# Attention and experts on one core: q and k in two float32r parts, two heads in the two row halves of TensorE, a new written-out order

## The reference

```python
qkv = x @ W_qkv                      # x: 16 x 1024 x 256
q, k = _rope(q, k)                   # per head: 1024 x 16
att = einsum('bhtd,bhsd->bhts', q, k) / sqrt(16) + causal mask
y = softmax(att) @ v                 # then heads side by side
x = layernorm(x + y @ W_o)
gate = softmax(x @ Wg + bg)          # top 2 of 8, renormalised
out = sum over experts of gate * (x @ We.T + be)
x = layernorm(x + out)
```

## Time and profile before

| what | us |
|---|---|
| median of 3 runs | 3425.34 (3417.21 to 3430.62) |
| the profiled execution | 3433.1 |
| its span | 3431.4 |
| PE busy in the span | 3291.5 (96%) |
| DVE busy | 2741.6 (80%) |
| ACT busy | 1897.2 (55%) |
| POOL busy | 1234.4 (36%) |

### The profile page before, as it was taken

How to read it: one execution, slowest core, us unless ns; L and a number is a source line. 1 busy time by engine, 2 the same in 40 slices (tenths; PEclk the granted TensorE clock), 3 DMA queues, 4 the chain that set the end, 5 groups by cost and what they waited for, 6 DMA issues and landing times.

```text
span 3431.4 us, 59169 instructions
## 1 busy us (share of the span) xinstructions
PE 3291.5 (96%) x19072; PEld 1738.4 (51%) x19072; DVE 2741.6 (80%) x8349; ACT 1897.2 (55%) x4257; POOL 1234.4 (36%) x1467
## 2 busy tenths in 40 slices
PE   5899999999999999999999999999999999999987
PEld 2234555555555555555555555555555555555555
DVE  5778887878888788888878888787888878888735
ACT  2367555564655556555564655657465564655541
POOL 4254324343333444334344332444334344432110
PEclk7799999999999999999999999999999999999998
DMA  5334343232433333343242433333343242434000
GB/s 135 59 61 81 52 84 56 45 79 48 83 52 68 59 58 70 52 84 57 50 79 42 83 57 74 57 55 69 58 78 57 52 75 50 77 52 72 2 25 13
DMA packets 174790, 210.98 MB, mean 61 GB/s; under 512 B 25992, under 2 KB 124560, under 8 KB 174224
## 3 DMA queue, kind: packets, MB, share of 16 engines
q1 hardware_dynamic: 173056, 202.98, 33.9%
q10 hardware_dynamic: 1424, 4.21, 0.3%
HBM read 138.43 MB, written 67.11 MB: 60 GB/s over the span
## 4 chain that ended last, share of the span: by engine, by line
PE 81%; DVE 9%; issue 3%; POOL 2%; DMA 2%; ACT 1%; DVEq 0%; ACTq 0%; SPq 0%; POOLq 0%
PE bank L890 22%; PE attend L983 15%; PE bank L947 13%; PE scores L963 13%; PE bank L927 6%; PE bank L1007 3%; PE bank L1045 2%; DVE bank L760 2%; PE bank L936 2%; DMA x_in<-in_x 2%; PE bank L991 1%; DVE maxima L763 1%; PE bank L915 1%; PE bank L998 1%; PE bank L1015 1%
## 5 line engine op out<-in xcount | busy, mean ns | idle before, releaser
L642 ACT ACTIVATE weights<-scores 128x512 f32<-128x512 f32 (+3 forms) x3072 | 1351.6, 494 | 1077.5 <-PE scores L963 1067.2
L760 DVE CUSTOM_DVE_ANT_0 bank<-bank,far_q 128x128 f32<-128x128 f32 (+3 forms) x2048 | 960.6, 514 | 217.2 <-PE bank L947 200.4
L963 PE MATMUL scores<-q_stack,k_stack 99*128 99x512 bf16 (+3 forms) x3072 | 826.1, 330 | 8.6 <-ACT weights L642 8.3
L947 PE MATMUL bank<-k_stack,q_stack 96*128 96x512 bf16 (+3 forms) x3072 | 792.6, 334 | 31.7 <-DMA k_stack<-parts_scratch 8.9
L559 POOL TENSOR_SCALAR_AFFINE_SELECT weights<-weights 128x512 f32<-128x512 f32 x512 | 325.3, 637 | 1201.7 <-ACT weights L642 1199.8
L763 DVE TENSOR_REDUCE maxima<-bank 128x1 f32<-128x512 f32 x1024 | 641.9, 682 | 49.0 <-PE bank L947 43.6
L983 PE MATMUL attend<-weights,v_now 128*32 128x512 f32 (+3 forms) x6144 | 660.9, 502 | 3.9 <-POOL weights L559 3.8
L963 PEld LDWEIGHTS scores<-q_stack,k_stack 99*128 99x128 bf16 x3072 | 265.7, 98 | 526.2 <-ACT weights L642 275.4
L947 PEld LDWEIGHTS bank<-k_stack,q_stack 96*128 96x128 bf16 x3072 | 271.2, 98 | 480.3 <-issue 242.2
L864 DVE SCALAR_TENSOR_TENSOR z<-bank,gates,z 128x256 f32<-128x256 f32 x512 | 247.0, 482 | 204.9 <-PE bank L890 203.6
L890 PE MATMUL bank<-wexp_hi,zT_hi 128*128 128x512 f32 x1024 | 377.2, 450 | 0.0
(11 more groups left out here) (106 smaller groups left out, 3467.2 us busy)
## 6 DMA issues: line engine op xcount, KB each, us to landing
parts_scratch<-parts SPq DMA_DIRECT2D x128, 384.0 KB, 2.5
q_stack<-parts_scratch SPq DMA_DIRECT2D x384, 128.0 KB, 7.1
k_stack<-parts_scratch SPq DMA_DIRECT2D x384, 128.0 KB, 7.6
x_in<-in_x SPq DMA_DIRECT2D x64, 256.0 KB, 3.0
z<-in_x SPq DMA_DIRECT2D x32, 512.0 KB, 5.1
out<-z SPq DMA_DIRECT2D x32, 512.0 KB, 3.4
q_stack<-maxrow SPq DMA_DIRECT2D x192, 8.0 KB, 2.1
z<-in_w_exp ACTq DMA_DIRECT2D x1, 1024.0 KB, 14.5
```

The source lines that it names most:

```text
L642: act.activation(weights[:, n % 2, hh, c0:CH], st[(QUAD * n + hh) % NS][:, c0:CH], ACT.Exp, scale=DH ** -0.5).then_inc(S["weights_ready"], 1)
L760: dve.tensor_tensor_reduce(out=b[:, 0:w], in0=b[:, 0:w], in1=far_q[:, CH - w:CH], scale=1.0, scalar=-SENTINEL, op0=ALU.add, op1=ALU.max, a ...
L947: pe.matmul(b[:, 0:w], q_stack[0:ROWS, n, hh, qt * P:(qt + 1) * P], k_stack[0:ROWS, n, hh, kc * CH:kc * CH + w], start=True, stop=True).th ...
L963: pe.matmul(st[(QUAD * n + hh) % NS][:, c0:CH], k_stack[0:MROWS, s, hh, kb * P:(kb + 1) * P], q_stack[0:MROWS, s, hh, qc * CH + c0:(qc + 1 ...
```

## The change

- Each of q and k is split into two float32r parts rather than three bf16 parts: one cast on ACT, one subtraction, which writes back into `rope`; both parts are stored, as float32, from `parts` and `rope`. The products are three rather than six: 48 rows and 2 rows of maxima, 50 rather than 99.
- A head therefore fits in 64 rows. The stacks hold heads 0 and 2 of a group in rows 0 to 63 and heads 1 and 3 in rows 64 to 127. `ST` uses the half `hh % 2`; `B` takes head `hh ^ 1`, so that it begins with the upper half.
- `LOAD` stays at 12 transfers, of 16 rows x 2 heads x 1024 float32. The maxima rows are split in two operations, not four, and written by 4 transfers, not 3.
- The copy of `QK` to `rope` waits for the store of the cast two before it, rather than for that cast's last subtraction.
- `ORDER` is written anew. Nearly every step moves by some places; maxima steps now stand more often in threes and fours, `MOE` steps in longer rows, `LOAD.0` one item earlier, `QK.1.0` seven items earlier.

The diff, cut to its core:

```diff
-TERMS = ((0, 0), (0, 1), (1, 0), (1, 1), (0, 2), (2, 0))
+TERMS = ((0, 0), (0, 1), (1, 0))
+PARTS = 2
 ROWS = len(TERMS) * DH
-MROWS = ROWS + 3
+MROWS = ROWS + PARTS
+LANE = 64
+LANES = P // LANE
+PAIRS = QUAD // LANES
...
-ST.16.0 ST.16.1 BE.0.0 ST.16.2 ST.16.3 B.1.3.1 CAST.0.3.1 B.1.3.2 B.1.3.3 PV.15 YE.1.0
-ST.17.0 B.1.4.0 ST.17.1 B.1.4.1 ST.17.2 BE.0.1 MOE.0.0.0 B.1.4.2 B.1.4.3 B.1.5.0 ST.17.3 PV.16
...
+ST.16.0 CAST.0.2 ST.16.1 ST.16.2 QK.0.3 B.1.3.3 ST.16.3 PV.15 B.1.4.0 B.1.4.1 B.1.4.2 YE.1.0
+ST.17.0 VP.2 VP.3 ROPE.0.3 GB.0 ST.17.1 B.1.4.3 B.1.5.0 B.1.5.1 ST.17.2 ST.17.3 PV.16 CAST.0.3 B.1.5.2 B.1.5.3
+  LOAD.1
+ST.18.0 ST.18.1 QK.1.0 B.1.6.0 ST.18.2 B.1.6.1 ST.18.3 PV.17 B.1.6.2 B.1.6.3 ROPE.1.0 B.1.7.0
+ST.19.0 GT.0 B.1.7.1 ST.19.1 ST.19.2 ST.19.3 PV.18 BE.0.0 BE.0.1 MOE.0.0.0 MOE.0.0.1 MOE.0.0.2 MOE.0.0.3
+  MOE.0.1.0 MOE.0.1.1 MOE.0.1.2
...
-        parts = sb("parts", [P, 2, 3, CH], BF16)
-        q_stack = sb("q_stack", [P, SLOTS, QUAD, T], BF16)
-        k_stack = sb("k_stack", [P, SLOTS, QUAD, T], BF16)
+        parts = sb("parts", [P, 2, CH], F32R)
+        q_stack = sb("q_stack", [P, SLOTS, PAIRS, T], F32R)
+        k_stack = sb("k_stack", [P, SLOTS, PAIRS, T], F32R)
...
-        def rest(eng, c, s, k, n):
...
+        def rest(eng, c, s, k):
+
+            eng.wait_ge(S["cast"], c.at("cast", ("CAST", s, k)))
+            eng.tensor_tensor(rope[:, k % 2].bitcast(F32R), rope[:, k % 2], parts[:, k % 2].bitcast(F32), ALU.subtract) \
+                .then_inc(S["parts_ready"], 1)
...
-                    sp.dma_start(dst[s * P:(s + 1) * P, :, ch * CH:(ch + 1) * CH], parts[:, k % 2]) \
-                      .then_inc(S[f"parts_stored{k % 2}"], DMA)
+                    dst = scratch[which].rearrange("a h d t -> a (h d) t")
+                    for part, src in enumerate((parts[:, k % 2].bitcast(F32), rope[:, k % 2])):
+                        sp.dma_start(dst[part, s * P:(s + 1) * P, ch * CH:(ch + 1) * CH], src) \
+                          .then_inc(S[f"parts_stored{k % 2}"], DMA)
...
+                            for i in range(LANES):
+                                row = LANE * i + DH * t
+                                src = scratch[which, parts_qk[which], QUAD * n + i:QUAD * (n + 1):LANES]
+                                sp.dma_start(stack[row:row + DH, n, :, :].bitcast(F32), src.rearrange("h d t -> d h t")) \
+                                  .then_inc(S[f"stack{n}"], DMA)
...
-                        act.wait_ge(S["parts_ready"], c.below("parts_ready", ("CAST", s, k, 1), 2))
+                        act.wait_ge(S[f"parts_stored{k % 2}"], c.below(f"parts_stored{k % 2}", ("CAST", s, k), 1, STORES))
...
-            dve.memset(k_stack[ROWS:MROWS, :, :, :], -1.0).then_inc(S["const_v"], 1)
+            for i in range(LANES):
+                minus = k_stack[LANE * i + ROWS // 32 * 32:LANE * (i + 1), :, :, :]
+                dve.memset(minus.bitcast(F32), -1.0).then_inc(S["const_v"], 1)
...
                     link(c, step, dve.tensor_copy(maxrow[:, 0], src))
-                    dve.tensor_tensor(maxrow_err[:, :], src, maxrow[:, 0], ALU.subtract).then_inc(fr, 1)
-                    emptied(dve, c, step)
-                    link(c, step, dve.tensor_copy(maxrow[:, 1], maxrow_err[:, :]))
-                    dve.tensor_tensor(maxrow[:, 2], maxrow_err[:, :], maxrow[:, 1], ALU.subtract) \
-                        .then_inc(S["maxrows_ready"], 1)
+                    dve.tensor_tensor(maxrow[:, 1], src, maxrow[:, 0].bitcast(F32), ALU.subtract).then_inc(fr, 1)
...
-                    pe.matmul(b[:, 0:w], q_stack[0:ROWS, n, hh, qt * P:(qt + 1) * P],
-                              k_stack[0:ROWS, n, hh, kc * CH:kc * CH + w], start=True, stop=True).then_inc(fu, 1)
+                    head = hh ^ 1
+                    low, pair = LANE * (head % LANES), head // LANES
+                    pe.matmul(b[:, 0:w], q_stack[low:low + ROWS, n, pair, qt * P:(qt + 1) * P],
+                              k_stack[low:low + ROWS, n, pair, kc * CH:kc * CH + w], start=True, stop=True).then_inc(fu, 1)
...
+                    low, pair = LANE * (hh % LANES), hh // LANES
+                    pe.matmul(st[(QUAD * n + hh) % NS][:, c0:CH],
+                              k_stack[low:low + MROWS, s, pair, kb * P:(kb + 1) * P],
+                              q_stack[low:low + MROWS, s, pair, qc * CH + c0:(qc + 1) * CH], start=True, stop=True) \
```

193 lines of the change are left out of this document (87 added, 106 removed).

## The result

The changed kernel is slower: 3572.6 us (median of 4 runs, 3565.5 to 3574.4) against 3427.4 us (now also of 4 runs), ratio 1.042 with an interval of 1.040 to 1.044. The span of its profiled execution is 3572.6 us too, 141.2 us more than the 3431.4 of before. The forecast was 3195 us.

What follows compares the result with a forecast made beforehand. PE's order of work was taken as the bound: a turn of 204.6 us, less 24.9 saved, plus 5.2 for shape changes and 5 idle, gives 189.9; over 15.75 turns, less 2 us in the opening, 3195 us, range 3105 to 3415.

Steps and rivals of the forecast that it cites:

- The bound and its reading: Middle-loop turn of 204.6 us: PE's order of work bounds it, busy 201.7 us; DVE second at 83%.
- The opening: Start of the span: DVE is the bound, nothing gained there; the copy of QK waiting for a store costs 2 us.
- Overlap of the halves: Score and maxima matmuls in opposite row halves load and stream together; a pair costs its wider member, 0.233 us at 512 columns.
- overlap in part: Rival for score and maxima pairs: each costs 1.16 of its wider member; turn 196.1 us, 3293 us; chance 0.13.
- loads one after another: Rival: the second weight load of a pair starts 0.11 us late; turn 200.8 us, 3367 us; chance 0.10.
- no overlap: Slower rival: halves don't run together, every matmul pays float32r; turn 217.7 us, 3633 us; chance 0.14.
- The saving: Score and maxima matmuls on PE: 38.9 us a turn instead of 63.8, so 24.9 us saved.
- the score tiles: Named risk without a size: pairs broken up by waits for the three score tiles might never start together.
- Changes of shape: Switches of PE array shape: 165 a turn instead of 108, 57 more at 0.09 us, adding 5.2 us.
- The added idle: PE waiting for DVE to read its four banks: 5 us more a turn.
- The clock: Read as 0.99 in the turns of the kernel before; the sum has no term for a change of it.
- the slower side: Slower rival at 3633 us, tied to halves not running together: chance 0.14; slower than before overall 0.17.

Runs made afterwards that it cites:

- same_half: Changed kernel with the x transposes moved off the turn's head and all heads read from the lower row half; 4061.9 us in one run.
- bf16_pairs: Changed kernel with two bf16 parts in place of two float32r parts, same row halves and order; 3415.6 us, 0.998 of before.
- four_tiles: Changed kernel with four score tiles and three other banks in place of three and four; 4075.7 us, 1.192 of before.
- full_array: Changed kernel with x transposes moved off the turn's head and score and maxima matmuls over 114 and 112 rows, not one half; 3608.7 us in one run.
- half_maxima: full_array with the maxima matmuls over the lower row half of 48 rows only, scores still over 114 rows; 4175.2 us in one run.

## Why the prediction was wrong

*In one sum.* The turn was forecast at 189.9 us and took 211.2, 21.3 more. The work at the full clock fell by 4.1 us and not by 19.7 (24.9 less 5.2): 15.6 of the 21.3. The low clock is 7.1 more. The idle gaps grew by 3.5 in place of 5: 1.5 less.

*The bound and its reading held.* PE was and stays the bound, and DVE, ACT and POOL lost what was forecast (3.3, 4.8 and 7.9 us a turn against 4.1, 5 and 9). The opening was mis-sized: from the start to the first long expert stretch the changed kernel lost 30 us where I had put 2. There is one wait for k_stack of 10.35 us, but the clock is also lower, 0.67 from 120 to 200 us where it was 0.90. The 70 us more at 1.2 GHz outside idle gaps cost up to 35 us, as much as the loss. No experiment took this apart.

*Overlap of the halves: right.* same_half shows it (1.14 us against 0.67 for four steps, 24 us a turn). The rivals of overlap in part, of loads one after another and of no overlap fell: two loads of different halves start within 0.01 us of each other.

*The saving: the term that failed first.* I costed the pairs at 38.9 us by their streaming. The runs that lie outside low stretches (358 of the 384 steps) take 58.2 us without idle gaps, the step out of each run included; pairs, 0.105 us for each entry and 0.093 for each exit come to 50.8. So the formula lacked the entry, 8.1 us a turn: rows of a steady stream hide the load behind the matmul before, and a run that begins with a change of shape has none. The same load in bf16 (98 ns) costs 0.01 us at this place, and bf16_pairs measures the difference directly. And it lacked 7.4 us inside the runs, 6.2 of them in runs of seven and more steps, where the last score matmul of an item wants a tile or a maxima matmul a bank. That these are waits is shown for the runs of seven alone (four_tiles). The two make 15.5 us, about what the work missed; the smaller terms aren't separated as finely. I named the score tiles as what could make me wrong, and gave it no term.

*Changes of shape: right in size, short in count of what they do.* They cost 0.09 us, and I counted 57 more. The steps on the other side of a change, projections and transposes, also show their float32 load: 44.7 us became 47.3. The first matmul of a QK step behind a score or maxima matmul took 0.43 us before and takes 0.53 now; in full_array, without the change of shape, it is 0.43 again.

*The added idle: 3.5 us against 5, from another place.* So this term came near by luck. It was the wait for x (3.1 us) and not DVE. The transposes at the head of the turn stand in the diff; I checked the loads of q and k and not these.

*The clock: not in the prediction at all.* I read 0.99 in the earlier trace rows and carried it over. Without the low clock the turn would be 202.4 us after and 203.0 before, 0.6 less. It has 15.9 us more of low clock, 14.1 of them outside idle gaps, and these cost the 7.1 us that make it 6.5 more. So the saving that failed took away the gain, and the clock decides the sign. same_half, full_array and half_maxima show that it comes with work in row halves. This was the missing rival on the slower side. The Trainium skill (TensorE: Matmul & The Clock Gate, HAM oscillation) tells of clock loss from idle gaps of PE. Here, full_array and same_half have gaps of 1.8 and 1.2 us a turn and clocks of 0.99 and 0.91; the gaps don't explain the difference, and the measurement decides.

The range ended at 3415 us and rested on a chance of 0.14 for the slower side, all of it tied to missing overlap. The gain had less margin than it seemed: 14.7 us a turn hung on 24.9 saved, and three terms of 7 to 8 us each, none of which shows in steady rows of the kernel before, were open.
